# A DMA queue and two engine programs reordered in the loop of a modulated attention kernel

## What is computed

```python
x = x + clip((x * style0) @ W0.T * demod0 + bias0, -256, 256)
kx = modulated_linear(x, s, k_aff_w, k_aff_b, k_w, k_b).reshape(B, N, 16, 32)
scores = jnp.einsum('bnhd,bnjd->bnhj', kx, kx) / math.sqrt(32)
A = jax.nn.softmax(scores, axis=-1)
out = jnp.einsum('bnhj,bnjd->bnhd', A, kx).reshape(B, N, 512)
x = x + modulated_linear(out, s, o_aff_w, o_aff_b, o_w, o_b)
```

## Time and profile before

| | |
|---|---|
| median of 3 runs | 739.38 us (739.37 to 746.77) |
| the profiled execution | 738.66 us |
| its span, first to last instruction | 736.9 us |
| busy: PE, DVE, ACT | 94%, 73%, 70% |
| TensorE clock granted | 0.983 of full |
| DMA: mean rate, share of the 16 engines in the loop | 213 GB/s, 0.83 |

### The profile page before, as it was taken

How to read it: one execution, slowest core, us unless ns; L and a number is a source line. 1 busy time by engine, 2 the same in 40 slices (tenths; PEclk the granted TensorE clock), 3 DMA queues, 4 the chain that set the end, 5 groups by cost and what they waited for, 6 DMA issues and landing times.

```text
span 736.9 us, 21634 instructions
## 1 busy us (share of the span) xinstructions
PE 693.7 (94%) x8886; PEld 673.5 (91%) x8886; DVE 538.0 (73%) x1048; ACT 517.2 (70%) x1040; POOL 4.3 (1%) x11
## 2 busy tenths in 40 slices
PE   7998988999999999999999999999998999989796
PEld 6998888899999999999899989989998999989685
DVE  3668766777778887677788767778876778877662
ACT  4786665767877776677777767778765777766673
POOL 2000000000000000000000000000000000000000
PEclk8999998999999999999999999999999999999999
DMA  9267897798879887888888779689778888876874
GB/s 291 82 172 183 223 238 167 198 240 231 234 220 249 227 205 200 229 230 227 234 227 233 207 201 237 203 242 234 199 199 225 235 229 230 231 194 154 221 217 131
DMA packets 235811, 157.16 MB, mean 213 GB/s; under 512 B 143297, under 2 KB 225217, under 8 KB 235713
## 3 DMA queue, kind: packets, MB, share of 16 engines
q1 hardware_dynamic: 235712, 155.78, 78.3%
HBM read 71.85 MB, written 67.11 MB: 189 GB/s over the span
## 4 chain that ended last, share of the span: by engine, by line
DMA 26%; PE 26%; SPq 17%; DVE 13%; ACT 12%; issue 5%; ACTq 0%; DVEq 0%
PE lin_ps L420 19%; DMA k_turned<-kx 9%; DMA k_bd<-k_rhs 8%; DMA yr<-y_turned 5%; PE s_ps L465 4%; SPq L247 4%; SPq L269 4%; SPq L237 4%; SPq L261 3%; DMA y_turned<-y 2%; ACT y_hi L516 2%; ACT kx L507 2%; ACT x_hi L516 2%; PE y_ps L483 2%; DVE x L761 2%
## 5 line engine op out<-in xcount | busy, mean ns | idle before, releaser
L420 PE MATMUL lin_ps<-x_hi,w_hi 128*128 128x256 f32 x1008 | 287.2, 285 | 5.7 <-DVE w_lo L712 3.5
L420 PE MATMUL lin_ps<-x_lo,w_hi 128*128 128x256 f32 x1008 | 283.0, 281 | 0.0
L420 PE MATMUL lin_ps<-x_hi,w_lo 128*128 128x256 f32 x1008 | 282.7, 281 | 0.0
L420 PEld LDWEIGHTS lin_ps<-x_hi,w_hi 128*128 128x128 f32 x1008 | 191.1, 190 | 13.1 <-issue 12.9
L420 PEld LDWEIGHTS lin_ps<-x_lo,w_hi 128*128 128x128 f32 x1008 | 191.2, 190 | 0.0
L420 PEld LDWEIGHTS lin_ps<-x_hi,w_lo 128*128 128x128 f32 x1008 | 191.2, 190 | 0.0
L420 PE MATMUL lin_ps<-y_hi,w_hi 128*128 128x256 f32 x528 | 150.2, 284 | 7.1 <-DVE y_lo L683 7.1
L420 PE MATMUL lin_ps<-y_lo,w_hi 128*128 128x256 f32 x528 | 149.1, 282 | 0.0
L420 PE MATMUL lin_ps<-y_hi,w_lo 128*128 128x256 f32 x528 | 149.0, 282 | 0.0
L516 ACT ACTIVATE x_hi<-x,style 128x256 fp32r<-128x256 f32 x252 | 113.1, 501 | 46.3 <-DVE x L761 39.5
L683 DVE SCALAR_TENSOR_TENSOR x_lo<-x,style,x_hi 128x256 fp32r<-128x256 f32 x252 | 107.1, 477 | 7.5 <-ACT x_hi L516 7.5
(11 more groups left out here) (59 smaller groups left out, 668.5 us busy)
## 6 DMA issues: line engine op xcount, KB each, us to landing
x<-xT SPq DMA_DIRECT2D x32, 512.0 KB, 7.3
k_turned<-kx SPq DMA_DIRECT2D x32, 512.0 KB, 4.4
k_st<-k_turned SPq DMA_DIRECT2D x128, 128.0 KB, 3.2
k_bd<-k_rhs SPq DMA_DIRECT2D x128, 128.0 KB, 5.0
v_turned<-k_rhs SPq DMA_DIRECT2D x32, 512.0 KB, 6.1
k_v<-v_turned SPq DMA_DIRECT2D x128, 128.0 KB, 3.3
y_turned<-y SPq DMA_DIRECT2D x128, 128.0 KB, 3.0
yr<-y_turned SPq DMA_DIRECT2D x32, 512.0 KB, 5.4
```

What stands on the lines that cost most here:

```text
L420: mm = pe.matmul(lin_ps[:, n % NLB, 0:T], w[:, k, m * P:(m + 1) * P], r[:, k, :], start=(q == 0), stop=(q == len(passes) - 1))
```

## The change

In the loop and in the tail's first round, the list of SP is put in another order. `load_x` moves from behind `y_from_dram` to behind `k_to_dram`, between the two hops of the keys, and loads chunk i + 1 instead of i + 2. `spread_k` and `store` (of chunk i - 5 instead of i - 4) move in front of `v_from_dram` and `y_from_dram`. The head loses `load_x(7)` and `store(1)`, which the loop now issues.

`normalise` is cut in two steps: `sums` (the sum and its reciprocal) and `normalise` (the product and the transpose). In the loop of DVE `turn_k` now stands right behind `sums`, in front of `make_x1` of the second half. Everywhere else the two steps stand together. In the loop of ACT the high parts of the next x and the evacuations of O come earlier, `spread_some` later, and the first `y_hi_of` stands one `k_out` later.

```diff
             for i in range(FIRST_LOOP, last - 1):
                 k_to_dram(i - 1)
+                load_x(i + 1)
                 k_from_dram(i - 1)
                 y_to_dram(i - 3)
+                store(i - 5, 0, 1)
+                spread_k(i - 1)
                 v_from_dram(i - 2)
                 y_from_dram(i - 3)
-                load_x(i + 2)
-                spread_k(i - 1)
                 v_to_dram(i - 1)
-                store(i - 4, 0, 1)
             k_to_dram(last - 2)
+            load_x(last)
             k_from_dram(last - 2)
             y_to_dram(last - 4)
+            store(last - 6, 0, 1)
+            spread_k(last - 2)
             v_from_dram(last - 3)
             y_from_dram(last - 4)
-            spread_k(last - 2)
             v_to_dram(last - 2)
...
-            def normalise(c):
+            def sums(c):
                 dve.wait_ge(a_exp, c + 1)
                 dve.tensor_reduce(out=total[:], in_=sc[:], axis=AX_X, op=ALU.add).then_inc(v_sum, 1)
                 dve.wait_ge(v_sum, c + 1)
                 dve.reciprocal(rcp[:], total[:]).then_inc(v_rcp, 1)
+
+            def normalise(c):
                 dve.wait_ge(v_rcp, c + 1)
```

More of the change, by code:

```diff
@@ L325, in _ @@
             v_from_dram(2)
-            load_x(7)
             y_to_dram(1)
@@ L808, in dve_steps @@
                 return [
-                    (c2, merge_scores), (c2, subtract_maxima), (c0, make_x1, 0), (c2, normalise), (c0, make_x1, 1),
-                    (c0, x1_lo_of, 0), (c1, turn_k), (c0, x1_lo_of, 1), (c2, spread_probabilities), (c4, finish, 0),
-                    (c2, turn_v), (c4, finish, 1), (i + 1, x_lo_of, 0), (i + 1, x_lo_of, 1), (c3, y_lo_of, 0),
-                    (c3, y_lo_of, 1)]
+                    (c2, merge_scores), (c2, subtract_maxima), (c0, make_x1, 0), (c2, sums), (c1, turn_k),
+                    (c0, make_x1, 1), (c0, x1_lo_of, 0), (c0, x1_lo_of, 1), (c2, normalise),
+                    (c2, spread_probabilities), (c4, finish, 0), (c2, turn_v), (c4, finish, 1), (i + 1, x_lo_of, 0),
+                    (i + 1, x_lo_of, 1), (c3, y_lo_of, 0), (c3, y_lo_of, 1)]
             dve_head = [
@@ L818, in _ @@
                 (O, weights_lo, 0), (2, make_x1, 0), (O, weights_lo, 1), (2, make_x1, 1), (3, x_lo_of, 0),
-                (3, x_lo_of, 1), (0, turn_k), (O, demod_of),
-                (2, x1_lo_of, 0), (2, x1_lo_of, 1), (3, make_x1, 0), (3, make_x1, 1),
-                (4, x_lo_of, 0), (4, x_lo_of, 1), (0, merge_scores), (0, subtract_maxima), (1, turn_k),
-                (0, normalise), (0, turn_v), (3, x1_lo_of, 0), (3, x1_lo_of, 1), (0, spread_probabilities),
-                (4, make_x1, 0), (4, make_x1, 1), (5, x_lo_of, 0), (5, x_lo_of, 1), (2, turn_k), (1, merge_scores),
@@ L824, in _ @@
-                (1, subtract_maxima), (1, normalise), (1, turn_v), (4, x1_lo_of, 0), (4, x1_lo_of, 1),
-                (1, spread_probabilities), (5, make_x1, 0), (5, make_x1, 1), (0, y_lo_of, 0), (0, y_lo_of, 1),
-                (2, merge_scores), (2, subtract_maxima), (3, turn_k), (2, normalise), (0, finish, 0), (6, x_lo_of, 0),
-                (6, x_lo_of, 1), (0, finish, 1), (2, spread_probabilities), (2, turn_v), (5, x1_lo_of, 0),
-                (5, x1_lo_of, 1), (1, y_lo_of, 0), (1, y_lo_of, 1), (3, merge_scores), (3, subtract_maxima),
@@ new lines, in _ @@
+                (3, x_lo_of, 1), (0, turn_k), (O, demod_of), (2, x1_lo_of, 0), (2, x1_lo_of, 1), (3, make_x1, 0),
+                (3, make_x1, 1), (4, x_lo_of, 0), (4, x_lo_of, 1), (0, merge_scores), (0, subtract_maxima),
+                (1, turn_k), (0, sums), (0, normalise), (0, turn_v), (3, x1_lo_of, 0), (3, x1_lo_of, 1),
+                (0, spread_probabilities), (4, make_x1, 0), (4, make_x1, 1), (5, x_lo_of, 0), (5, x_lo_of, 1),
+                (2, turn_k), (1, merge_scores), (1, subtract_maxima), (1, sums), (1, normalise), (1, turn_v),
@@ new lines, in _ @@
+                (4, x1_lo_of, 0), (4, x1_lo_of, 1), (1, spread_probabilities), (5, make_x1, 0), (5, make_x1, 1),
+                (0, y_lo_of, 0), (0, y_lo_of, 1), (2, merge_scores), (2, subtract_maxima), (3, turn_k), (2, sums),
+                (2, normalise), (0, finish, 0), (6, x_lo_of, 0), (6, x_lo_of, 1), (0, finish, 1),
+                (2, spread_probabilities), (2, turn_v), (5, x1_lo_of, 0), (5, x1_lo_of, 1), (1, y_lo_of, 0),
+                (1, y_lo_of, 1), (3, merge_scores), (3, subtract_maxima), (3, sums), (3, normalise), (1, finish, 0),
```

43 lines of the change are left out of this document (21 added, 22 removed).

## The result

| | changed kernel | kernel before, same chip |
|---|---|---|
| median | 763.87 us (762.09 to 767.23, 4 runs) | 743.08 us (739.37 to 747.21, 4 runs) |
| ratio | 1.035, 95% interval 1.030 to 1.041 | |
| the profiled execution, its span | 765.43, 763.6 us | 738.66, 736.9 us |

What follows compares the result with a forecast made beforehand. It took PE's own round, 20.76 us per loop iteration, as the floor, with 14.7 us of waiting. 738.66 - 3.9 (loop) + 3.4 (tail) = 738.2, plus 0.7 for the median: 738.9 us, no change; range 728 to 753.

Steps and rivals of the forecast that it cites:

- What bounds the kernel now: Loop: PE's unstalled iteration of 20.76 us is the floor; 14.7 us of waiting is the most to gain.
- What the change takes away: Loop: the wait of `scores` for the spread goes, up to 14.7 us; x in the gap and `store` cost nothing.
- Rival 3: Loop, DVE: late key reads make `turn_k` hold x1 back and PE stops ahead of K; 742 to 746; chance 0.09.
- (b), the circle: Loop: key write, reads, turn, spread's and values' issues, results' read, high part, evacuation in a row: 20.8 us against PE's 20.76.
- the rule weighed there: Fit for a DMA on GpSimd's path: 2.0 us plus bytes over 436e3, 3.2 us for 512 KB.
- The bound on record: Loop, slow bound: results' read 5.6 and key write 4.3 give a circle of 22.2 us, +19.9 on the loop.
- Rival 2: Loop: the circle, 21.5 us with a results' read of 5.6, is the bound; 747.9 us; chance 0.20.
- its long form, 763: Loop: Rival 2 with the long key write as well, 763 us.
- (a), the values: Loop: values issued behind the spread are transposed by +17.0 to +18.4, while `pv` starts at +17.1; no room left.
- the ring: Loop: another word for the circle, the steps from one key write to the next, forecast at 20.8 us.
- (c), the tail: Tail's first round: later values delay x's low parts, a 3.1 us stall before L0 of chunk 31; +3.4 us, bounds 2.6 to 5.
- The head: Head: 0.5 us of issue and one transfer go, but PE waits for other steps; 0, at most -1.

Runs made afterwards that it cites:

- the last experiment: Changed kernel with the spread between the two reads (behind both in the tail's first round) and both results' high parts behind K's last evacuation: 723.37 us, ratio 0.974.
- the experiment with the swap: Changed kernel with both high parts of the results behind the last evacuation of K in ACT's loop: 737.95 us, ratio 1.002.

## Why the prediction was wrong

**What bounds the kernel now: right.** The floor of 20.76 per iteration was met to 0.1 us in the whole loop by the last experiment, and 14.7 us was the most that there was to win: before's 512.9 less 498.3 is 14.6. Only its make-up was read loosely: the 15.6 us of the earlier trace rows are the weight load's wait, PE's own was 11.6, and the rest is PE busy 2.9 us longer than in that loop.

**What the change takes away: right.** The wait for the spread is gone, and the engine lists alone remove 5.0 of PE's 11.6 us. That x in the gap costs nothing holds for the round as a whole, though the key reads are 0.27 us longer with it; the store's issue costs nothing, since the queue still stands idle for 0.8 us in the mean before the spread. Rival 3 shows only at the edge: PE's 1.1 us of waits for `x_hi`, in two iterations, stand ahead of layer K.

**(b), the circle: the step that failed.** Its members and their order were right, and `pv` pays, as said. Wrong was its length: 20.8 in the forecast, 22.18 in the result. The excess comes from three terms: results' read +0.6, key reads +0.6, spread's issues +0.2. The results' read was put at 4.9, "nearer the loop's", though the one row for it in the loop said 5.6 in the middle; for going below it (x gone from behind) there was no row. The forecast also counted the values in front as new, where they stood in front of it before. The key reads were put at 4.8 from one iteration; over the 24 rounds of the loop before they took 5.03 in the mean from the key write's landing to the last, and 5.44 now, with x in front. Only the key write, for which a crowded and a free row were both weighed, came out.

Of the rule weighed there, from the Trainium skill, page "DMA: Bandwidth & Descriptors", section "Anatomy of one DMA — SWDGE (gpsimd) path", the trace shows that it doesn't carry over to a read on this queue in a loaded loop: 3.2 us by its fit, 5.50 in the mean and 4.4 at the least in the changed loop.

The rest of the failure is what a wrong length does here. The forecast took a circle as long as PE's round and charged scatter, 0.45 us per iteration. A ring that is longer pays its whole excess in each of 24 rounds: 24 x (22.18 - 20.76) = 34.1 us over the floor of 498.2, where the loop is 35.4 over it. The bound on record (22.2, +19.9 on the loop) is what came: +20.7. That it fits so closely is in part luck: it has the key write at 4.3, which was 3.63, and the key reads at 4.8, which were 5.44, and the same kernel gave 755.73 us on the other chip. Rival 2 named the mechanism and the point at which it decides, a results' read of about 5.3; it was 5.50 on the one chip, where the kernel lost 3.5%, and 5.28 on the other, where it lost 1.9%. A chance of 0.20 was too low for a case on whose side the only row of the loop lay, and its long form, 763, near which the result came (763.87), was left outside the range.

**(a), the values: right in direction.** They come just in time or late, and it is through them that the ring reaches PE. In the experiment with the swap, 9.3 us of waits for them are left in 7 iterations.

**What was not in the sum at all: the clock.** Of the +20.7 in the loop 7.1 are PE busy longer. This isn't added to the ring's excess, since the ring sets the length either way. The second profile of the changed kernel bears this out: it has no stretch at half clock in the loop (PE busy for 500.4 us), and its loop is still 24.3 us over the floor, where 24 x (21.85 - 20.76) is 26.2. In the tail, where no ring repeats, it does add.

**(c), the tail: right stall, wrong sum.** 3.1 us forecast for the stall ahead of chunk 31's L0, 3.9 measured; the tail as a whole 3.4 forecast, 9.7 measured (7.8 in the second profile of the changed kernel). PE's idle time there grew by 4.6 us (16.1 to 20.7) and its busy time by 5.1 (75.3 to 80.4), by the same view of both kernels; the second goes with more time at half clock, 20.1 us where it was 8.2, most of it at waits of 2.5 to 3.9 us. "No row shows anything later in the tail that would take it back" was true; that something would add to it was not asked. By the groups of tails above the spread's order costs about 4 us, within the bounds on record (2.6 to 5). The other 4 go with the load of the last x, which the change puts into that round and which the forecast put at nothing in the tail. The two make up the difference of the groups' means, 100.0 and 91.9; the 9.7 of this pair of profiles is that and scatter.

**The head** was put at 0, at most -1, and gave 3.7 in this pair of profiles. The two kernels with the old head take 132.6 us each, the twelve others 127.5 to 130.8, so the head does gain some 3 us, more than the forecast allowed. Which of its two DMAs that went gives it was not tested; in the two kernels that load x later, with `load_x(7)` back and `store(1)` still gone, it is 130.0 and 127.5, which points at the store without showing it.

## What to carry to other kernels

When a step is moved forward on an in-order queue, write down the whole ring from one iteration's step to the same step in the next, through every engine and queue that it passes, and compare its length with the round of the engine that sets the pace. Take each landing from loaded rows of the loop, not from isolated ones, and if the ring comes out within a few per cent of the round, count the case in which it is longer as the likely one: the excess is paid in every iteration, the gain is taken once. Write down the queue's own issuing as a second path beside the chain of waits: with the spread between the reads it became the ring, and the forecast that left it out was 1 us short. If the ring is too long, cut it at the cheapest link, which need not be near the change: here swapping two short ACT instructions was worth 13 us or more in the loop, and with the spread between the two reads as well the kernel is 2.6% faster than before (2.0 to 3.2).

## What the runs showed of the hardware

- **A wait can cost more than itself.** In the changed loop, five waits of PE of 2.0 to 2.8 us were each followed by some 3.4 us at a granted clock near 0.5; in the tail a wait of 3.9 us was followed by about 5.6 us of it. It isn't so behind each wait of that length: none followed 2.5 us in the same loop, 2.6 in the loop before, or 3.1 and 3.2 in the loop with the late turn. PE's busy time for the loop's 6533 matmuls was 498.3 us without waits, 500.4 with 21.7 us of them and no stretch at half clock, 508.3 with 24.9 us of them, and 515.6 with 59.0 us. (A busy PE's ends are modelled, but the four are modelled alike.)
- **A 512 KB read takes longer in the loop than alone, and its neighbours on the queue matter.** The results' read took 3.7 us alone and, in loops, in the mean 4.9 to 5.2 with the spread between it and the values, 5.3 to 5.6 in the changed order, 5.5 and 5.95 in the old order with x and then the spread behind it, and 6.8 with the spread right behind it. x right behind it adds nothing that shows in the one pair with all else alike (5.05 and 5.10).
- **Issues are in the ring too.** Four small DMAs hold the SP queue for 2 to 3 us in the mean (2.7 for the spread, 2.2 for the values). More than a fifth of the ring, 4.9 of 22.2 us, was the queue issuing, not data moving; with the spread between the reads it was over half, 11.3 of 21.0.
